# Zero fill by the engines, and gathers that wait for the landing of the one two places ahead

## The reference, cut to what matters

```
n   = layernorm(x)
s   = n @ W_sc * z            # per node, in four parts of 64 columns
h   = n @ W_lin1 * z          # per node: the table that the edges read
hid = silu(edge_attr_8 @ fc_w0 / sqrt(8));  w = hid @ fc_w1 / 8      # per edge
xs  = h[src]                                                          # gather, 256 floats per edge
mid = products of w, xs and edge_attr_4                               # 512 floats per edge
y   = segment_sum(mid, dst) / 4
x   = x + sin(pi/8) * s + cos(pi/8) * (y @ W_lin2) * z
x   = x + shared_expert(layernorm(x)) + routed_experts(layernorm(x))  # 8 experts, top 2, width 1024
```

## Time and profile before

| what | value |
|---|---|
| median of 3 runs | 1373.57 us (1373.14 to 1381.37) |
| the profiled execution | 1377.12 us |
| its span, first to last instruction | 1375.2 us |
| mean granted clock of PE | 0.895 |
| PE, DVE, ACT, POOL busy | 85, 56, 53, 46% of the span |
| DMA | 141.64 MB, mean 103 GB/s |

### The profile page before, as it was taken

How to read it: one execution, slowest core, us unless ns; L and a number is a source line. 1 busy time by engine, 2 the same in 40 slices (tenths; PEclk the granted TensorE clock), 3 DMA queues, 4 the chain that set the end, 5 groups by cost and what they waited for, 6 DMA issues and landing times. The chain is left out here.

```text
span 1375.2 us, 31654 instructions
## 1 busy us (share of the span) xinstructions
PE 1175.3 (85%) x8904; PEld 1008.7 (73%) x8904; DVE 769.0 (56%) x1951; ACT 726.8 (53%) x2357; POOL 634.2 (46%) x695
## 2 busy tenths in 40 slices
PE   5667888788888888878878887999799999999993
PEld 4445666667766666656756677999799999999993
DVE  5634555555555545545555567644357666676652
ACT  4535766566756656655746666445344444444431
POOL 4565555545545545445444510355224444455443
PEclk9869888878979888878888898999899999999997
DMA  8652323323323333323333336223324344443222
GB/s 292 191 163 82 103 72 114 115 82 105 99 92 105 95 99 111 105 86 110 97 92 93 98 109 216 89 77 112 102 59 101 54 97 105 108 105 73 43 40 31
DMA packets 86943, 141.64 MB, mean 103 GB/s; under 512 B 14926, under 2 KB 65422, under 8 KB 86480
## 3 DMA queue, kind: packets, MB, share of 16 engines
q0 software_dynamic: 31840, 67.39, 20.1%
q1 hardware_dynamic: 51104, 69.90, 15.2%
q10 hardware_dynamic: 3920, 3.41, 0.8%
HBM read 99.48 MB, written 30.95 MB: 95 GB/s over the span
## 5 line engine op out<-in xcount | busy, mean ns | idle before, releaser
L748 POOL DMA_INDIRECT x_wlo<-h_tab,src_sb x392 | 376.5, 960 | 365.0 <-DVE hot L897 155.3
L779 ACT ACTIVATE hots<-hot,sh_all 128x64 f32<-128x64 f32 x1568 | 383.9, 336 | 0.0
L1103 PE MATMUL psY<-prod,hots 128*64 128x128 f32 x2352 | 345.9, 311 | 13.1 <-issue 12.4
L1103 PEld LDWEIGHTS psY<-prod,hots 128*64 128x64 f32 x2352 | 312.9, 160 | 28.0 <-issue 28.0
L1099 PE MATMUL psY<-prod,hots 128*64 128x256 f32 x784 | 273.4, 472 | 10.4 <-issue 10.1
L925 DVE SCALAR_TENSOR_TENSOR y_sb<-psY,mask,y_sb 128x256 f32 x196 | 85.7, 478 | 264.9 <-remote 235.0
L1864 ACT ACTIVATE q_hf<-q_psA,x_b 128x256 f32<-128x256 f32 x232 | 110.2, 475 | 186.7 <-PE q_psA L1380 166.5
L1087 PE MATMUL psW<-fc_w,hid 64*128 64x256 f32 x784 | 154.5, 447 | 63.6 <-issue 51.7
L769 ACT ACTIVATE hid<-psE 128x256 f32<-128x256 f32 x98 | 37.3, 380 | 279.3 <-remote 140.5
L1087 PEld LDWEIGHTS psW<-fc_w,hid 64*128 64x128 f32 x784 | 83.3, 204 | 121.4 <-issue 89.8
L1807 POOL DMA_INDIRECT out_rows<-q_ob,q_index x56 | 91.4, 1633 | 152.0 <-issue 98.0
(11 more groups left out here) (243 smaller groups left out, 2253.6 us busy)
## 6 DMA issues: line engine op xcount, KB each, us to landing
x_raw<-in_w SPq DMA_DIRECT2D x18, 1024.0 KB, 6.0
x_wlo<-h_tab,src_sb POOLq DMA_INDIRECT x392
u_y<-y_sb SPq DMA_DIRECT2D x11, 512.0 KB
y_sb<-y_sb SPq DMA_DIRECT2D x2, 2176.0 KB, 13.8
x_sb<-in_x SPq DMA_DIRECT2D x5, 640.0 KB, 6.0
h_tab<-x_raw ACTq DMA_DIRECT2D x5, 640.0 KB, 4.9
base_d<-s_sb SPq DMA_DIRECT2D x5, 640.0 KB, 3.7
cols_hi<-xT_d SPq DMA_DIRECT2D x5, 640.0 KB, 4.4
```

The source lines that it names most:

```text
L748: pool.indirect_dma_start(out=rows[t % RING][:, c, :, :].rearrange("p a u -> p (a u)"), out_offset=None, in_=h_tab, in_offset=bass.Indirec ...
L779: ins = nc.scalar.activation(hots[p][:, c, n, :], hot[p][:, c, :], ACT.Copy, scale=sh_all[:, at(j), c, n:n + 1].rearrange("p o n -> p (o n)"))
L1103: ins = nc.tensor.matmul(side[:, k::3 - k, :][:, 0:2, :], hots[p][:, c, k + 1, :], prod[p][:, c, 4::k + 1, :][:, 0:2, :], start=(c == 0 an ...
```

## The change

In the node stage SP no longer copies zeros. In the edge stage POOL sets the middle 17 blocks of `y_sb` to zero (128x4352) ahead of its waits for `h_tab`, ACT copies the first 17 onto the last 17 behind its first table load, and DVE waits for both before its first turn. Of the gathers, c = 0 keeps its wait for the products of step t-4; the two other waits go, and each gather from the third on waits for the landing of the one two places ahead of it (BEHIND = 2). `row_in` is now counted per c and not per step, so DVE waits four times per step, with an increment behind each. SP's load of the first weights waits for the radial of step 3 (`w_done`, which starts at 2).

```diff
--- before.py
+++ after.py
@@ -211,7 +211,7 @@
         based, base_go = sem("based"), sem("base_go")
         consts, wzero, zscaled, fczero = sem("consts"), sem("wzero"), sem("zscaled"), sem("fczero")
         pool_step, dve_step = sem("pool_step"), sem("dve_step")
-        span_done, y_zero = sem("span_done"), sem("y_zero")
+        span_done = sem("span_done")
         passed = sem("passed")
         x_ready, stats_done, aggr_done, root_done = sem("x_ready"), sem("stats_done"), sem("aggr_done"), sem("root_done")
         rstd_done = sem("rstd_done")
@@ -246,10 +246,6 @@
                 sp.dma_start(w0[NB * half:NB * (half + 1), MUL * half:MUL * (half + 1)], v["fc0"][0:NB, 0:MUL]
                              ).then_inc(fc_in, 16)
 
-            sp.wait_ge(pool_step, 11)
-            for i in range(2):
-                first = BLOCKS + 2 - ZERO * (i + 1)
-                sp.dma_start(y_sb[:, first:first + ZERO, :], y_sb[:, 0:ZERO, :]).then_inc(y_zero, 16)
             sp.wait_ge(span_done, 1)
             sp.dma_start(span_d, span[:]).then_inc(span_out, 16)
             for g in range(1, NG):
@@ -275,7 +271,6 @@
                              s_sb[:, GROUP * g:GROUP * (g + 1), :]).then_inc(base_out, 16)
             sp.wait_ge(fc_in, 16 * 6)
             sp.wait_ge(tab_in, 48)
-            sp.wait_ge(y_zero, 32)
 
         @block.gpsimd
         def _(pool):
@@ -523,6 +518,8 @@
     AWAY = 8192
     PIECE = WW // ITER
     MOST = PAIR + 1
+    ZERO = (BLOCKS + 2) // 3
+    BEHIND = 2
     assert T - ITERS * ITER == 2 and PAIR == 2 and CHUNK * 2 == ITER and NT == 2 * ITERS + 1
 
     with ExitStack() as ctx:
@@ -580,7 +577,7 @@
         z_out = sem("z_out")
         dve_step, pool_step = sem("edve_step"), sem("epool_step")
         e_in = [sem(f"ee_in{i}") for i in range(2)]
-        row_in = [sem(f"row_in{i}") for i in range(ITER)]
+        row_in = [sem(f"row_in{c}") for c in range(C)]
         hid_done, silu_done = sem("hid_done"), sem("silu_done")
         w_done, prod_done, hot_done = sem("w_done"), sem("prod_done"), sem("hot_done")
         hots_done, seg_done, y_done = sem("hots_done"), sem("seg_done"), sem("y_done")
@@ -595,7 +592,7 @@
         scored, logits_out = sem("u_scored"), sem("u_logits_out")
         rows_out, rows_free, cols_out, cols_free = (sem(n) for n in ("u_rows_out", "u_rows_free", "u_cols_out",
                                                                      "u_cols_free"))
-        u_go = sem("u_go")
+        u_go, y_zero = sem("u_go"), sem("y_zero")
         block = ctx.enter_context(nc.Block())
         LAST = ITERS - 1
 
@@ -679,7 +676,7 @@
             sp.wait_ge(h_out[0], 16 * (NG // 2 + 2))
             sp.wait_ge(h_out[1], 16 * (NG // 2 + 1))
             sp.wait_ge(base_out, 16 * NG)
-            sp.wait_ge(row_in[2], 16 * C)
+            sp.wait_ge(w_done, 2 + 4)
             load_w1(sp, raw, v["w1"], 0, w_in)
             load_w2(sp, raw, v["w2"], 0, w_in)
             sp.dma_start(x_end[:], base_d.rearrange("(t p) f -> p t f", p=P)[:, NT - MOST:, :]).then_inc(x_end_in, 16)
@@ -731,6 +728,7 @@
         @block.gpsimd
         def _(pool):
             link = chain_of(pool, pool_step)
+            pool.memset(y_sb[:, BLOCKS + 2 - 2 * ZERO:BLOCKS + 2 - ZERO, :], 0.0).then_inc(y_zero, 1)
             pool.wait_ge(h_out[0], 16 * (NG // 2 + 2))
             pool.wait_ge(h_out[1], 16 * (NG // 2 + 1))
             R = pool.value_load(rounds_i[0:1, 0:1], min_val=1, max_val=BLOCKS + 2)
@@ -740,15 +738,14 @@
                     for c in range(C):
                         if c == 0:
                             pool.wait_ge(prod_done, (r * T + max(t, RING - 1)) * 2 + 2)
-                        if c == 1 and t >= RING - 2:
-                            pool.wait_ge(hot_done, r * T + t - RING + 3)
-                        if c == 2:
-                            pool.wait_ge(prod_done, (r * T + t) * 2 + 3)
+                        if t * C + c >= BEHIND:
+                            pool.sem_inc(gather_turn, 1)
+                            pool.wait_ge(row_in[(c - BEHIND) % C], 16 * (r * T + (t * C + c - BEHIND) // C + 1))
                         pool.sem_inc(gather_turn, 1)
                         pool.indirect_dma_start(
                             out=rows[t % RING][:, c, :, :].rearrange("p a u -> p (a u)"), out_offset=None, in_=h_tab,
                             in_offset=bass.IndirectOffsetOnAxis(ap=src_sb[:, t, c:c + 1], axis=0),
-                        ).then_inc(row_in[t % ITER], 16)
+                        ).then_inc(row_in[c], 16)
             link(pool.memset(blank[:], 0.0))
             link(pool.memset(empty[:], 0))
             link(pool.iota(empty[:, :, 0], [[0, PLACES]], base=NPAD, channel_multiplier=1))
@@ -848,6 +845,7 @@
 
 
             nc.scalar.activation(warm[:], iota_row[:, 0:1], ACT.Silu)
+            nc.scalar.activation(y_sb[:, BLOCKS + 2 - ZERO:, :], y_sb[:, 0:ZERO, :], ACT.Copy).then_inc(y_zero, 1)
             act.sem_inc(silu_done, 2)
             act.sem_inc(hots_done, 2)
             act.sem_inc(yT_ready, 1)
@@ -905,7 +903,9 @@
 
                 dve.wait_ge(seg_done, r * T + j + 1)
 
-                dve.wait_ge(row_in[q], 16 * C * (r * USES[q] + k + 1))
+                for c in range(C):
+                    dve.wait_ge(row_in[c], 16 * (r * T + j + 1))
+                    dve.sem_inc(u_go, 1)
                 w, x, out_p = psW, rows[q % RING], prod[p]
                 nc.vector.tensor_tensor(out_p[:, :, 0:3, :], w[:, :, 2:3, :].to_broadcast([P, C, 3, MUL]),
                                         x[:, :, 1:4, :], ALU.mult)
@@ -1035,6 +1035,7 @@
                 step(nc.vector.tensor_scalar(window[:], window[:], float(SPAN), None, ALU.add))
                 step(nc.vector.tensor_scalar(block_f[:], block_f[:], 1.0, None, ALU.add))
                 one_hot(r, 0, 0)
+                dve.wait_ge(y_zero, 2)
                 for q in range(ITER):
                     turn_of(r, 0, q)
                 for q in range(ITER):
```

## The result

The changed kernel took 1368.76 us (median of 18 runs, 1365.77 to 1373.72), the kernel before 1374.18 (18 runs, 1368.13 to 1386.66): ratio 0.9946, 95% interval 0.9929 to 0.9963. That is 5.4 us faster, within the 1% that was called no change, where 1288 was forecast. One thing has to be known to read the experiments: the kernel before does not take the same time on every chip. On five of the seven chips of the experiments it took 1129 to 1134 us (medians), on the two others 1379 and 1388, as in the trace ahead of the prediction. Each experiment is therefore given with the kernel before on its own chip.

The account below looks back on a forecast made before the run. The edge stage was taken as bound by gathers in flight starving PE. From the profiled 1377.1 us, -86 (gathers), -3 (zero fill) and +3 (late first products) gave 1291, less 3.5 for the median: 1288 us; 8-in-10 range 1262 to 1460.

Parts of the forecast that it names:

- That gathers in flight starve PE, and that a steady wider distance ends it: Edge stage: bursts of gathers hold PE back; gathers evenly 1.70 us apart would leave it no longer starved.
- the term 98 x (6.8 - 7.68) = -86 us: Edge stage, 98 steps: paced gathers would set the step at 6.8 us in place of 7.68, gaining 86 us.
- The distance of two gathers: POOL, edge stage: a gather and the one two later 2.96 to 3.47 us apart, taken as 1.70 a gather.
- the sign of being right: Changed profile, POOL: gather starts 1.5 to 1.75 us apart on average would show the forecast right.
- The zero fill: Node stage: without SP's two DMAs copying zeros, a gain of 0 to 3.6 us, taken as -3.
- the memset with late first products: Start of edge stage: POOL's memset costing 2 us and a later fourth gather delay DVE's first products, +3 in all.
- The cycle only changes its shape: Rival, chance 0.12: DVE's L910 waits for landings instead of L925 for "remote"; step 7.68 +-0.1, 1362 to 1385 us.
- Longer bursts: Rival, chance 0.32: PE is free only with no gather in flight, so longer bursts make it slower, 1404 to 1498 us.
- Its deciding point: Slower rival: PE would be freed only from a gather distance of 2.66 us, the time to a landing.
- Half of the stall stays: Rival, chance 0.17: "remote" keeps half of its 235.0 us at DVE's add; step 7.2 us, 1327 us.
- Issue early, wait late: Skill rule cited against waiting for landings at the gathers: early issue and late wait overlap a transfer's fixed cost; no size.
- DVE's four waits: DVE ahead of L910: four waits and increments per step, hidden at 0, or +15 us if uncovered.

Follow-up runs that it names:

- e11_half: Kernel before with the new zero fill, no waits at c = 1 and 2, a small memset and wait ahead of every second gather; starved chip: 1260.5 us, ratio 0.9133.
- e10: Changed kernel with BEHIND = 1, one gather in flight at a time: 2059.03 us (one run).
- e4: Kernel before with the new zero fill, no waits at c = 1 and 2, a small memset and wait ahead of each gather: 1378.69 us.
- e1_zero: Kernel before with the zero fill of the change alone, gathers keeping their old waits: 1123.73 us, ratio 0.992.
- e5_after: The changed kernel itself on a chip where the kernel before took 1129.44 us: 1361.18 us, ratio 1.2031.
- e15: Kernel before with the zero fill of the change alone, repeated beside a kernel before of 1132.19 us: 1122.86 us, ratio 0.9914.
- e18: Kernel before with the zero fill of the change alone, repeated beside a kernel before of 1131.41 us: 1124.9 us, ratio 0.9943.
- e16_behind3: Changed kernel with BEHIND = 3, on a starved chip where the kernel before took 1388.04 us: 1440.07 us, ratio 1.0384.
- e2_pace: Kernel before with the gathers' part of the change alone, SP still copying zeros: 1377.53 us, ratio 1.2161.
- e9: Changed kernel with BEHIND = 4, each gather waiting for the landing of the one four ahead: 1144.28 us, ratio 1.0094.
- e8_before: The kernel before, unchanged, against itself on a chip where it took 1134.35 us: 1134.18 us, ratio 0.9999.

## Why the prediction was wrong

**That gathers in flight starve PE, and that a steady wider distance ends it: right,** where a chip starves at all. The remote waits at the add went from 235.0 us to none, as forecast, and in e11_half to 18.5 without a landing waited for. The distance of 1.58 us in the mean is enough; with BEHIND = 3, at mostly 1.26 us, it is not.

**The step that failed is the term 98 x (6.8 - 7.68) = -86 us.** Measured as the prediction measured it before, from the first gather to the end of the last add, the edge stage is (810.8 - 58.4) / 98 = 7.68 us a step: the term came out at -1. Three things make up the 86 us.
- The distance of two gathers was put between 2.96 and 3.47 us and taken at 3.4. The median is 3.56, that is 7.12 us a step, and 98 x (7.12 - 6.80) = 31 us. The prediction's own rows had it: they give a landing after 2.66 to 2.76 us and 0.81 behind it, and 2.76 + 0.81 is 3.57; the "at most" of 3.47 was added up from the smaller one. And between the two ends no choice was open, since a release by a landing costs the 0.8 each time (e10: landing 2.75, start to start 3.55).
- Landings are not all alike. The mean of two is 3.77, not 3.56, so the gathers took 739.6 / 98 = 7.55 us a step: 42 us more. (That is 1.89 us a gather, where 1.5 to 1.75 was named as the sign of being right.) The rows had a landing in a quiet stretch, and e10 and e4 show 2.75 us beside nothing and 3.83 and 4.08 beside much other traffic. That the traffic is the reason rests on these hundreds of gathers; no run took it away. A kernel whose every gather waits pays the mean of its landings, where an unpaced one hides the late ones.
- The 6.8 is a pace of gathers, the 7.68 a whole stage by 98, with the steps that follow the last gather. These took 752.4 - 739.6 = 13 us in the changed kernel, which a sum of gathers leaves out. From first start to last the gathers took 733.8 / 98 = 7.49 us a step before, so even 6.8 would have gained only 67 us.

**That the times are nearly equal is a coincidence.** Before, the starved PE set the pace, after, the landings do; 7.49 and 7.55 us a step have nothing in common, and on chips without starvation the gathers go from 498 us (e1_zero) to 738 (e5_after).

**The sign of the small result** was forecast for another reason. The zero fill was put at -3 and the memset with late first products at +3; the first gather came 6.8 us earlier. Alone the zero fill measured 6.5 to 9.3 us (e1, e15 and e18, ratios 0.9914 to 0.9943), all on chips that aren't starved. The memset cost nothing: from POOL's last add of the node stage (57.90, now 51.01) to the first gather it is 7.3 us before and 7.4 after. From the first gather to DVE's first product it is 8.1 us after 6.9, 1.2 of the 3. Two DMAs on SP had a price at the release of the loaded tiles, which the two terms named didn't hold. The gathers' part is +5.8 - 6.9 = -1.1 us in the two profiled executions, so the zero fill makes most of the gain, as far as single executions tell. It wasn't measured alone on a starved chip.

**Rivals.** "The cycle only changes its shape", put at 1362 to 1385 with DVE's L910 waiting for a landing what L925 waited for "remote", describes the outcome word for word; it had 0.12. Its "7.68 +-0.1" is not worked out from any row, so that it met the time is luck; that DVE would wait for rows in place of "remote" is what it had right. "Longer bursts" did not happen to the change, but to e16_behind3: 1440.07 us, with bursts that only the buffers end; that lies in its 1434 to 1498, but at another distance and beside a kernel before of 1388.04, so its sum isn't borne out by it. Its deciding point, a distance of 2.66 us, was wrong: with BEHIND = 2 nine in ten of the distances are 1.26 to 2.45 us, so that a gather is nearly always in flight, and PE isn't starved. "Half of the stall stays" did not happen: none stayed.

**Issue early, wait late.** The rule of the Trainium skill's "DMA: Bandwidth & Descriptors", Rules for kernel authors, to issue a DMA early and wait on its semaphore late, was named against the change and set aside. It is borne out: where PE isn't starved the waits for landings cost 245 us (e2_pace), and each landing from issue to next start 3.55 us (e10).

**DVE's four waits, the weights.** DVE's have the waits for rows to hide behind in the changed kernel; in e9 they may be part of 20 us. The weights' share was not told apart.

**What stays open:** why two chips of seven starve PE under dense gathers and five don't, with the same program and the same 0.95 us of POOL per gather. The DMA engines don't tell them apart: between 100 us and the end of the gathers a packet of the gathers' queue takes 0.154 us in the mean both in the kernel before's first trace and in e8_before. No run bears on the cause, and why dense gathers hold PE back at all is as open. That it was such a chip could not be told from the one trace ahead of the prediction. What the zero fill alone and the unpaced gathers do on a starved chip was not measured.

## What to carry to other kernels

Before a wait for a landing is put into a loop, multiply the time from issue over landing to next issue, under the loop's own traffic and not in a quiet stretch, by the number of transfers and divide by those in flight: if that is more than the loop takes, the wait becomes the bound. Compare it with the same quantity before, gathers with gathers and not with a stage. If transfers are to be spread out, a fixed small delay does it at the distance chosen, and costs little beyond it (e4: 752.7 us, where 392 x 1.89 is 741). A stall that the trace puts down to "remote" can belong to the chip: run the kernel before on more than one chip before a change is built upon it.

## What the runs showed of the hardware

The kernel before takes 1129 to 1134 us on five chips and 1379 and 1388 on two, with one and the same program, and executions of one chip stay in one form: of 7 on one chip 1372.46 to 1384.07, of 13 on another 1128.9 to 1137.9.

Dense indirect gathers can starve PE, and with it DVE and ACT: on the starved chips 1.26 us apart they do (235.0 and 284.7 us of remote waits at DVE's add), 1.26 and 1.89 in turn they hardly do (18.5 us). In the kernel before each of the 40 remote waits ended 2.0 to 4.5 us after the start of the last gather of its burst, 2.7 in the median.

A landing seen by POOL costs 3.55 us from start to start, whether one or two are in flight (medians 3.55 and 3.56), of which 2.75 are from start to landing (the gather's own work on POOL, 0.95, is in them) and 0.8 from there to the next start. Beside other transfers that fill over 40% of the DMA engines' time the landing is 3.8 to 4.1 us in the median.

DVE's first instruction of the edge stage (128x98) took 3.74 us beside POOL's memset of 3.73, starting 0.04 us later and ending with it. It took 3.74 in every trace with the memset, and 0.21 in the three without: both of the kernel before, and e2_pace, which is the changed kernel without the zero fill:

```profile
61.47 0.21 DVE L884 TENSOR_SCALAR window<-first_node 128x98 f32<-128x98 f32 x1 [0.54 <-PEq L157]
```

ACT's copy, the other part of the zero fill, starts only 2.8 us after DVE's instruction, which speaks for the memset as what holds it. It cost nothing here, since DVE's first product waited for rows.
